# Layer 0's attention: q/k stored by head, loads moved to SyncE, short units in fp32, values three units behind

## The reference, cut to what matters

```python
q, k, v = (proj(Wq), proj(Wk), proj(Wv))          # [B, 16, 1024, 32]
q = q * cos + rotate_half(q) * sin
k = k * cos + rotate_half(k) * sin
scores = jnp.einsum('bhqd,bhkd->bhqk', q, k) / math.sqrt(HD)
scores = jnp.where(causal, -jnp.inf, scores)
attn = jax.nn.softmax(scores, axis=-1)
out = jnp.einsum('bhqk,bhkd->bhqd', attn, v)
return jnp.einsum('bsh,oh->bso', out, Wo)
```

## Time and profile before

| | us |
|---|---|
| timed runs, median (lowest, highest), 3 runs | 3482.31 (3478.21, 3484.29) |
| profiled execution, its own time | 3477.39 |
| its span | 3475.6 |
| PE busy | 2886.4 (83% of the span), mean granted clock 0.922 |
| DVE, ACT, POOL busy | 2013.0, 1203.2, 952.2 |
| attention of layer 0, first load to last scaling | 197.6 to 740.5 |

### The profile page before, as it was taken

One profiled execution on the slowest core, in us unless ns is written; L12 is line 12 of the kernel. 1 busy time (PEld: TensorE's weight loads), 2 busy tenths in 40 slices (PEclk: granted clock), 3 DMA queues, 4 the chain that ended last, 5 costly groups with the idle time before them and its releaser, 6 DMA issues. The chain is left out here.

```text
span 3475.6 us, 42242 instructions
## 1 busy us (share of the span) xinstructions
PE 2886.4 (83%) x14636; PEld 2297.1 (66%) x14636; DVE 2013.0 (58%) x3642; ACT 1203.2 (35%) x2343; POOL 952.2 (27%) x664
## 2 busy tenths in 40 slices
PE   7948887876999999248899999589999994488994
PEld 6835555554888888237688888477888883366773
DVE  5638787855222222435566666655666666767655
ACT  2216565532111111113344444224444442233331
POOL 1216666653111111204100000140000001267733
PEclk9969899987999999679999999799999996699997
DMA  4542232222001000671100000300000003111002
GB/s 161 201 151 79 80 94 84 72 68 97 19 19 37 18 0 1 213 283 74 37 21 32 21 32 27 148 22 16 32 21 32 25 24 113 57 37 37 0 1 97
DMA packets 111744, 224.36 MB, mean 65 GB/s; under 512 B 9377, under 2 KB 55457, under 8 KB 110849
## 3 DMA queue, kind: packets, MB, share of 16 engines
q1 hardware_dynamic: 95472, 183.92, 15.2%
q10 hardware_dynamic: 16144, 38.80, 3.7%
HBM read 155.84 MB, written 66.58 MB: 64 GB/s over the span
## 5 line engine op out<-in xcount | busy, mean ns | idle before, releaser
L1043 POOL TENSOR_TENSOR l0a_probs_hl<-l0a_probs,l0a_probs_hl 128x896 fp32r<-128x896 f32 (+1 forms) x128 | 293.6, 2314 | 213.8 <-ACT l0a_probs L958 213.8
L1275 PE MATMUL l1a_obank<-l1a_pT_hl,l1k_v_hl 128*128 128x512 f32 (+3 forms) x1152 | 300.1, 369 | 7.1 <-DVE l1a_pT_hl L1348 7.1
L1348 DVE TENSOR_TENSOR l1a_pT_hl<-l1a_work,l1a_pT_hl 128x512 fp32r<-128x512 f32 (+3 forms) x384 | 213.1, 555 | 154.2 <-ACT l1a_pT_hl L1308 154.0
L1301 ACT ACTIVATE l1a_probs<-l1a_scores,l1a_row 128x128 f32<-128x128 f32 (+7 forms) x256 | 189.7, 742 | 318.0 <-DVE l1a_row L1338 318.0
L1255 PE MATMUL l1a_scores<-l1k_kT_hl,l1a_qa_hl 128*128 128x512 f32 (+3 forms) x1152 | 291.7, 362 | 1.5 <-ACT l1a_probs L1301 1.5
L1391 POOL TENSOR_TENSOR l1a_q_stage<-l1k_qpe,l1a_ones 128x512 fp32r<-128x512 f32 x32 | 33.4, 1043 | 873.9 <-PE l1a_work L1283 816.7
L1680 DVE TENSOR_TENSOR f0f_hid<-f0f_silu,f0f_ubank 128x512 f32<-128x512 f32 x64 | 44.0, 688 | 322.0 <-PE f0f_ubank L1615 322.0
L957 ACT ACTIVATE l0a_probs_hl<-l0a_sbank 128x896 fp32r<-128x896 f32 (+1 forms) x192 | 156.2, 814 | 190.3 <-PE l0a_sbank L904 127.3
L1308 ACT CAST l1a_pT_hl<-l1a_work 128x512 fp32r<-128x512 f32 (+3 forms) x384 | 183.7, 478 | 104.8 <-PE l1a_work L1266 103.6
L1283 PE MATMUL l1a_work<-l1a_wov,l1a_oT_hl 128*128 128x512 f32 x768 | 211.9, 398 | 5.0 <-DVE l1a_oT_hl L1367 3.0
L1338 DVE TENSOR_REDUCE l1a_row<-l1a_scores 128x1 f32<-128x128 f32 (+7 forms) x256 | 189.9, 751 | 44.5 <-PE l1a_scores L1258 44.2
(11 more groups left out here) (254 smaller groups left out, 6270.6 us busy)
## 6 DMA issues: line engine op xcount, KB each, us to landing
qk_dram<-l0f_stage SPq DMA_DIRECT2D x8, 2048.0 KB, 9.4
l1a_wov<-wov_dram SPq DMA_DIRECT2D x32, 512.0 KB, 3.4
v_dram<-l0f_v_rows SPq DMA_DIRECT2D x16, 768.0 KB, 3.7
l0a_v_stage<-v_dram ACTq DMA_DIRECT2D x8, 1536.0 KB, 19.6
l1a_wabs<-wabs_dram SPq DMA_DIRECT2D x32, 384.0 KB, 3.9
l0a_q_stack<-qk_dram ACTq DMA_DIRECT2D x32, 256.0 KB
l0a_k_stack<-qk_dram ACTq DMA_DIRECT2D x32, 256.0 KB
wov_dram<-w1a_wov SPq DMA_DIRECT2D x16, 512.0 KB, 3.3
```

What stands on the lines that cost most here:

```text
L1043: nc.gpsimd.tensor_tensor(probs_hl[:, r, 1, 0:wide], probs[:, r, 0:wide], f32(probs_hl[:, r, 0, 0:wide]), ALU.subtract).then_inc(low_done[ ...
L1275: last = pe.matmul(obank[:, c:SPAN], src["v_hl"][:, a, n, :], pT_hl[:, ring(n, s), b, c:SPAN], start=(n == 0 and i == 0), stop=(n == QT * ...
L1301: nc.scalar.activation(probs[s][:, first:first + wide, :].rearrange("p k c -> p (k c)"), scores[:, n % S_AHEAD, 0:wide * P], ACT.Exp, bias ...
L1348: nc.vector.tensor_tensor(pT_hl[:, r, 1, c:SPAN], work[:, slot, c:SPAN], f32(pT_hl[:, r, 0, c:SPAN]), ALU.subtract).then_inc(work_free[slo ...
```

## The change

1. `qk_dram` is laid out by head: for each, 32 high rows next to 32 low ones. SP stores a pair of tiles by 16 DMAs of 128 KB where it was one of 2048 KB. The load of high and low rows becomes one contiguous block.
2. Stacks, values and the output weights are loaded from SP's queue instead of ACT's. Values come in quarters of two key tiles, one per head, and the output weights at head 4.
3. For the key tiles 2, 3, 6 and 7 the values are also kept in plain fp32 (`v32_dram`, `v32_stage`). Units 1 and 5 multiply `probs` by these in fp32 matmuls, without high and low parts: one exponential and no subtraction for them. DVE makes no low parts any more.
4. Values run three steps behind (`LAG`), the ring of weights grows from 4 to 6 slots, and the order in a step is Z, N, L, P, O, M, M.

```diff
             def store_pair(pair):
                 b, first = divmod(2 * pair, TB)
                 sp.wait_ge(low_done, use["K", 2 * pair + 1] + 1)
-                rows = qk_dram[b].rearrange("w l g p s -> p (w l g) s")[:, :, first * P:(first + 2) * P]
-                sp.dma_start(rows, f32(stage[:, pair % 2].rearrange("p w l g s -> p (w l g) s"))).then_inc(qk_stored[pair % 2], 16)
+                cols = slice(first * P, (first + 2) * P)
+                for w in range(2):
+                    for part in range(2):
+                        for j in range(GROUP_HEADS):
+                            sp.dma_start(qk_dram[b, w, :, j, part, :, cols].rearrange("g d s -> d g s"),
+                                         f32(stage[j * HD0:(j + 1) * HD0, pair % 2, w, part])).then_inc(qk_stored[pair % 2], 16)
...
+                if tt in KT_FP32:
+                    sp.wait_ge(v32_made, made_upto(t))
+                    sp.dma_start(v32_dram[b, :, KT_FP32.index(tt)].rearrange("g p c -> p g c"),
+                                 v32_rows[:, t % 2].rearrange("p (g j) c -> p g (j c)", g=KT)).then_inc(v32_stored[t % 2], 16)
...
+                    if t % TB in KT_FP32:
+                        wait(act, v32_stored[t % 2], 16 * ((made_upto(t) - 1) // 2))
+                        nc.scalar.copy(v32_rows[:, t % 2, :, 2 * HD0:3 * HD0], in_heads(t)).then_inc(v32_made, 1)
...
+                nc.vector.memset(v32_rows[:, slot, :, 0:HD0], 0.0).then_inc(ones_set, 1)
+                nc.vector.memset(v32_rows[:, slot, :, HD0:2 * HD0], 1.0).then_inc(ones_set, 1)
...
+LAG = 3
+RING0 = LAG + 3
 QW = 3 * HD0
 KW = QW + 2
 UNITS = [(0, (0, 1)), (0, (2, 3)), (1, (0, 1)), (1, (2, 3)), (1, (4, 5)), (1, (6, 7))]
 U = len(UNITS)
-FIRST, LAST = -2 * U, HEADS * U + 2
+FIRST, LAST = -2 * U, HEADS * U + LAG + 1
 MAX_PARTS = [(t, c) for t in range(TB) for c in range(0, (t + 1) * P, SPAN)]
-LOWS_BY_DVE = (1, 5)
+IN_FP32 = (1, 5)
+KT_FP32 = [kt for kt in range(TB) if kt % QT >= 2]
...
     for i in range(FIRST, LAST):
         h, k = divmod(i, U)
+        if 0 <= i + 2 < HEADS * U:
+            yield "Z", i, i + 2
         if k == 0 and 0 <= h + 1 < HEADS:
             yield "N", i, h + 1
-        if 0 <= i + 2 < HEADS * U:
-            yield "Z", i, i + 2
+        if 0 <= i < HEADS * U:
+            yield "L", i, i
+        p, o = i - LAG, i - LAG - 1
+        if 0 <= p < HEADS * U:
+            yield "P", i, p
+        if 0 <= o < HEADS * U and o % U in (1, U - 1):
+            yield "O", i, 2 * (o // U) + (o % U == U - 1)
         if h + 2 < HEADS:
             yield "M", i, 2 * (h * U + 2 * U + k)
             yield "M", i, 2 * (h * U + 2 * U + k) + 1
-        if 0 <= i < HEADS * U:
-            yield "L", i, i
-        if 0 <= i - 1 < HEADS * U:
-            yield "P", i, i - 1
-        if 0 <= i - 2 < HEADS * U and (i - 2) % U in (1, U - 1):
-            yield "O", i, 2 * ((i - 2) // U) + ((i - 2) % U == U - 1)
...
+            def load_stack(h):
+                b, g, j = h // NH, h % NH // GROUP_HEADS, h % GROUP_HEADS
+                slot = h % STACKS
+                if h >= STACKS:
+                    sp.wait_ge(scores_full, (h - STACKS + 1) * U)
+                both = lambda w: qk_dram[b, w, g, j].rearrange("l d s -> (l d) s")
+                sp.dma_start(f32(q_stack[0:2 * HD0, slot, :]), both(0)).then_inc(stack_loaded[slot], 16)
+                sp.dma_start(f32(q_stack[2 * HD0:QW, slot, :]), qk_dram[b, 0, g, j, 0]).then_inc(stack_loaded[slot], 16)
+                sp.dma_start(f32(k_stack[0:HD0, slot, :]), qk_dram[b, 1, g, j, 0]).then_inc(stack_loaded[slot], 16)
+                sp.dma_start(f32(k_stack[HD0:QW, slot, :]), both(1)).then_inc(stack_loaded[slot], 16)
+
+            def load_values(group, quarter):
+                b, g = divmod(group, KT)
+                slot, kts = group % 2, slice(2 * quarter, 2 * quarter + 2)
+                if group >= 2:
+                    sp.wait_ge(values_done, (group - 1) * GROUP_HEADS * U)
+                sp.dma_start(f32(v_stage[:, slot, kts].rearrange("p t j c -> p t (j c)")),
+                             v_dram[b, g, kts].rearrange("t p c -> p t c")).then_inc(v_loaded[slot], 16)
+                if quarter == 0:
+                    sp.dma_start(v32_stage[:, slot].rearrange("p t j c -> p t (j c)"),
+                                 v32_dram[b, g].rearrange("t p c -> p t c")).then_inc(v_loaded[slot], 16)
...
+            for first in range(STACKS - 1):
+                load_stack(first)
...
-                if k == 3 and 0 <= h - 1 < HEADS:
+                if h == -1 and k == 3:
+                    for quarter in range(4):
+                        load_values(0, quarter)
+                    load_stack(STACKS - 1)
+                if k == 4 and 0 <= h and h + STACKS < HEADS:
+                    load_stack(h + STACKS)
+                group, quarter = divmod(h, GROUP_HEADS)
+                if k == LAG + 2 and 0 <= group and group + 1 < GROUPS:
+                    load_values(group + 1, quarter)
+                if h == GROUP_HEADS and k == 0:
+                    sp.dma_start(*next_load).then_inc(next_loaded, 16)
+                if k == LAG + 2 and 0 <= h - 1 < HEADS:
                     store_sums(h - 1)
...
-                    mine, count = lows_upto(n)
-                    pe.wait_ge(low_done[mine], count)
+                    if u in IN_FP32:
+                        pe.wait_ge(exp_done, n + 1)
+                    else:
+                        pe.wait_ge(low_done, lows_upto(n))
                     for kt, c, at, _ in parts:
-                        for part in range(2):
-                            last = pe.matmul(obank[0:3 * HD0, s, c:SPAN],
-                                             v_stage[:, group % 2, kt, j, :],
-                                             probs_hl[:, r, part, at:at + SPAN - c], start=(kt == 0 and part == 0),
-                                             stop=(kt == QT * (s + 1) - 1 and part == 1))
+                        span = slice(at, at + SPAN - c)
+                        if u in IN_FP32:
+                            steps = [(v32_stage[:, group % 2, KT_FP32.index(kt), j, :], probs[:, r, span])]
+                        else:
+                            steps = [(v_stage[:, group % 2, kt, j, :], probs_hl[:, r, part, span]) for part in range(2)]
+                        for part, (values, weights) in enumerate(steps):
+                            last = pe.matmul(obank[0:3 * HD0, s, c:SPAN], values, weights, start=(kt == 0 and part == 0),
+                                             stop=(kt == QT * (s + 1) - 1 and part == len(steps) - 1))
                     last.then_inc(values_done, 1)
...
-            def load_stack(h):
-                b, g, j = h // NH, h % NH // GROUP_HEADS, h % GROUP_HEADS
-                slot, rows = h % STACKS, slice(j * HD0, (j + 1) * HD0)
-                if h >= STACKS:
-                    act.wait_ge(scores_full, (h - STACKS + 1) * U)
-                act.dma_start(f32(q_stack[0:2 * HD0, slot, :]), qk_dram[b, 0, :, g, rows, :]).then_inc(stack_loaded[slot], 16)
-                act.dma_start(f32(q_stack[2 * HD0:QW, slot, :]), qk_dram[b, 0, 0, g, rows, :]).then_inc(stack_loaded[slot], 16)
...
-            load_stack(0)
-            load_stack(1)
-            load_stack(2)
-            load_values(0)
-            load_stack(3)
-            load_values(1)
-            act.dma_start(*next_load).then_inc(next_loaded, 16)
...
-                    nc.scalar.activation(probs_hl[:, r, 0, 0:wide], sbank[:, n % 2, 0:wide], ACT.Exp)
+                    if n % U not in IN_FP32:
+                        nc.scalar.activation(probs_hl[:, r, 0, 0:wide], sbank[:, n % 2, 0:wide], ACT.Exp)
                     nc.scalar.activation(probs[:, r, 0:wide], sbank[:, n % 2, 0:wide], ACT.Exp).then_inc(exp_done, 1)
-                    h, u = divmod(n, U)
-                    if u == U - 1 and h + STACKS < HEADS:
-                        load_stack(h + STACKS)
-                    group, rest = divmod(n - 1 - 4, U * GROUP_HEADS)
-                    if rest == 0 and 1 <= group and group + 1 < GROUPS:
-                        load_values(group + 1)
-            act.wait_ge(next_loaded, 16)
...
-                elif kind == "L" and n % U in LOWS_BY_DVE:
-                    _, _, wide = pieces(n % U)
-                    r = n % RING0
-                    dve.wait_ge(exp_done, n + 1)
-                    nc.vector.tensor_tensor(probs_hl[:, r, 1, 0:wide], probs[:, r, 0:wide],
-                                            f32(probs_hl[:, r, 0, 0:wide]), ALU.subtract).then_inc(low_done[True], 1)
...
-                if kind == "L" and n % U not in LOWS_BY_DVE:
+                if kind == "L" and n % U not in IN_FP32:
                     _, _, wide = pieces(n % U)
                     r = n % RING0
                     pool.wait_ge(exp_done, n + 1)
                     nc.gpsimd.tensor_tensor(probs_hl[:, r, 1, 0:wide], probs[:, r, 0:wide],
```

(2 more changed lines are left out.)

52 lines of the change are left out of this document (25 added, 27 removed).

## The result

3425.8 us median (3422.3 to 3430.9, 4 runs) against 3480.3 (3476.9 to 3484.3, 4 runs): ratio 0.9844, 95% interval 0.9827 to 0.9862, some 54 us less where 88 were forecast. The profiled execution took 3422.3 around a span of 3420.6.

What follows compares the result with a forecast made beforehand. No engine full: layer 0's attention was bound by its slow start, a ring of waits per plain head, and disturbed heads. 4 - 9.9 - 3.3 - 17.4 - 2.3 - 59.0 = -87.9 us gave 3394; range 3363 to 3432.

Steps and rivals of the forecast that it cites:

- rival 1: Layer 0 heads: PE's wait before N (one transpose per head) eats more, head 14.1 us, total 3427; chance 25%.
- Front, +4 (+2 to +8): Before layer 0's attention: 16 stores per pair add 2.5 us, four memsets ahead of DVE's weight splits 1.5.
- Stacks, -9.9 and -3.3: Attention start: contiguous loads spread over 16 DMA engines, first stack ready 9.9 us sooner; 3.3 us wait for the second goes.
- Queue, -17.4: Head 1 to 2: loads on SP free ACT for its first exponential, 30.43 us becomes 13.0.
- The plain head, 13.0: Undisturbed attention head, N to N: new order and fp32 units bring 14.07 us to 13.0, with DVE setting the pace.
- Disturbed heads become plain: Heads 3 to 31: lag 3 and ring of 6 make all 28 heads take 13.0 us, saving 59.0.
- Rival 3: Attention heads: the clock falls every head after PE's stand, +42 us, total 3436; chance 8%.
- Rival 2: Attention heads: DVE's output steps slip into its pauses, PE leads, head nears 12.0 us, total 3364; chance 13%.

Runs made afterwards that it cites:

- e5: Changed kernel with one store per pair of tiles in the earlier layout and six 32-row loads a stack, all on SyncE: 3412.7 us, ratio 0.9801.
- e6: Changed kernel with the earlier q/k layout, one store a pair and four loads a stack, loads still on SyncE: 3514.4 us, ratio 1.0100.
- e12: Changed kernel with values one step behind instead of three and the ring back from 6 to 4 slots: 3385.9 us, ratio 0.9750.
- e1: Changed kernel with DVE's reciprocal of a group's sums two steps earlier: 3416.6 us, ratio 0.9824.
- e2: Changed kernel with POOL's two multiplications by the inverse sums one step later: 3407.0 us, ratio 0.9802.
- e3: Changed kernel with both moves, reciprocal two steps earlier and POOL's multiplications one step later: 3405.1 us, ratio 0.9787.
- e7: On top of e3, units 1 and 5 again as high and low, with low parts made by DVE, lag 3 kept: 3536.6 us, ratio 1.0157.
- e4: Changed kernel with N placed behind the value matmuls (P) of its step in PE's order: 3408.6 us, ratio 0.9791.
- e14: Changed kernel with short units' low parts by DVE and values one step behind, keeping storage, loads and new step order: 3449.9 us, ratio 0.9943.

## Why the prediction came out as it did

The direction was right and the time lies in the range; the value was 32 us low. That the range held is in part luck: 3425.8 is 6 us under its upper end, which was drawn to take in rival 1's 3427, and rival 1's mechanism is not what happened. By N(31), 652.1 against 617.4 forecast:

- *Front, +4 (+2 to +8)*: measured +9.6, beyond the bound. The last of the 16 issues goes out some 15.6 us later than the single one did, not 7.5; attention starts 2.3 us behind its end, as said. By e5 the issues are 3.0 us of the 9.6. The eight fp32 stores, put at 0, are the likely rest: their bytes come at the front's end, where the DMA engines are full.
- *Stacks, -9.9 and -3.3*: held, 9.7 and 3.0; 5.7 us to the first stack against 5.5 forecast, no wait for the second. By e6 the layout was worth far more, 89 us: it also carries the maxima past the bulk.
- *Queue, -17.4*: mechanism held, size 2.6 too large: head 1 to 2 took 15.58, as PE still ran at clock 0.50 until 244. Head 2 to 3: 12.93, held.
- *The plain head, 13.0*: measured 12.93. DVE was busy 9.65 (bound given: 9.9), the stand before N 1.42 (1.8). The sum was right, but it held the price of lag 3 unnamed: "the second output step now between them 1.4". I took the lag as free, and never summed the head with lag 1; it measures 12.05 (e12).
- *"Disturbed heads become plain"*: this is the step that failed, 26 of the 35 us. It put the disturbance down to POOL's delay of the low parts and to the DMA of row maxima. Both went, and others stood behind them: a reciprocal in DVE's run to N, a join held until POOL's multiplications end, and a fall of the clock behind each of these long stands (e1, e2, e3). I had said that nothing in DVE's run to N has slack, and did not look for what else runs there once in a group. The trace of before showed it, inside the very head that was taken as plain, where it cost nothing (14.07, as in the heads without it):

```profile
456.52 0.35 DVE L976 RECIPROCAL l0a_sums<-l0a_sums 128x32 f32<-128x32 f32 x1
```

- *Rivals*: rival 1's figure, 3427, is the measured one, but only its place was right; the plain head did not grow. Rival 3's fall of the clock came, in two heads of four, behind stands of 1.80 and 2.57 us and not behind 1.42. Rival 2's 12.0, by output steps that slip into DVE's pauses, is what lag 1 gives. In the trace of before, L1004's 1.86 us beside POOL's low parts (from 449.92 on) was the sign of the lock: the same operation takes 0.55 alone (e7).

## What to carry to other kernels

A deeper lag is not free: it moves everything that hangs on the late stage, here DVE's output step, and may put it into the run that sets the pace; sum the loop with each part of a change alone. Once a plain period is right, list what runs once in several periods on the pace-setting engine, and place it in a pause; where a stand is long enough to bring the clock down, 0.35 us can cost 1.7, as here. A short DVE operation with both operands in SBUF should not meet a long POOL instruction.

## What was not expected of the hardware

- DVE's 128 x 4 join took 1.30 and 1.45 us beside POOL's 1.2 and 2.3 us instructions, ending with them, and 0.16 otherwise; its 384-wide subtraction 1.74 against 0.55.
- The granted clock kept 1.00 behind stands of 1.42 us, fell to 0.50 behind 2.55, and behind 1.80 it fell in six of seven heads of the changed kernel and in four of seven in e2. In other kernels it fell behind 0.86 (three times in e4) and 1.74 (e12), and kept 1.00 behind 1.65 (e4) and behind some of 2.05 (e14).
- SyncE's 16 issues of 128 KB took 11.24 us, 0.70 each, with the DMA engines at 0.98; the same queue's stack loads took 0.41 to 0.59 each.
